# Last layer's dense experts on one Trainium2 core: the down product as three one-pass products on high and low parts, in two banks in turn

## The reference, cut to what matters

```
def _ffn(x, w1, b1, w2, b2):
    h = jax.nn.gelu(x @ w1.T + b1)          # 128 -> 512
    return h @ w2.T + b2                    # 512 -> 128
logits = xf @ router_w.T + router_b
routing = softmax(logits); sel_w, sel_idx = top_k(routing, 2); sel_w = sel_w / sel_w.sum()
comb = zeros_like(routing).at[rows, sel_idx].set(sel_w)
shared_out = _ffn(xf, shared_w1, shared_b1, shared_w2, shared_b2)
for each of 8 experts: acc = acc + comb[:, e] * _ffn(xf, w1_e, b1_e, w2_e, b2_e)
return shared_out + acc
```

## Time and profile before

| | |
|---|---|
| median of 3 runs | 1499.58 us |
| profiled execution, its own time | 1501.9 us |
| its span, first to last instruction | 1500.1 us |
| busy in the span: PE, DVE, ACT, POOL | 1155.9, 956.0, 681.9, 587.5 us |
| granted TensorE clock, mean of the span | 0.875 |
| down products (L1748), 288 matmul records | 152.1 us busy |
| up products (L1826), 432 matmul records | 217.8 us busy |

### The profile page before, as it was taken

How to read it: one execution, slowest core, us unless ns; L and a number is a source line. 1 busy time by engine, 2 the same in 40 slices (tenths; PEclk the granted TensorE clock), 3 DMA queues, 4 the chain that set the end, 5 groups by cost and what they waited for, 6 DMA issues and landing times.

```text
span 1500.1 us, 12998 instructions
## 1 busy us (share of the span) xinstructions
PE 1155.9 (77%) x3838; PEld 562.7 (38%) x3850; DVE 956.0 (64%) x2178; ACT 681.9 (45%) x1299; POOL 587.5 (39%) x404
## 2 busy tenths in 40 slices
PE   3226758859695959679697777878997899999897
PEld 1002323323232323324233433535454455555553
DVE  5976789688977788565857778665636634433321
ACT  6424543375436553152323525425553358554443
POOL 1880676328551767112103654363524111112111
PEclk7556778979697979769798999989998899999999
DMA  5000000000000000200001000000000200000000
GB/s 201 0 0 1 0 1 0 1 0 1 1 0 1 0 1 1 96 0 0 0 1 63 2 1 1 1 0 1 0 2 0 64 1 1 7 1 8 1 8 7
DMA packets 11270, 17.76 MB, mean 12 GB/s; under 512 B 1304, under 2 KB 7584, under 8 KB 10688
## 3 DMA queue, kind: packets, MB, share of 16 engines
q1 hardware_dynamic: 11200, 16.93, 3.4%
HBM read 15.88 MB, written 1.05 MB: 11 GB/s over the span
## 4 chain that ended last, share of the span: by engine, by line
PE 40%; DVE 11%; ACT 4%; issue 3%; POOL 2%; POOLq 0%; DVEq 0%; ACTq 0%
PE bankE L1748 8%; PE bankE L1826 6%; PE bankE L1247 3%; PE bankS L1790 2%; PE bankE L1309 2%; PE bankS L1775 2%; PE bankE L1268 1%; PE bankE L601 1%; PE bankS L1728 1%; DVE c_tw L1918 1%; PE bankE L523 1%; PE bankE L560 1%; ACT b_pr L1145 1%; PE bankE L1297 1%; PE bankE L594 1%
## 5 line engine op out<-in xcount | busy, mean ns | idle before, releaser
L1748 PE MATMUL bankE<-c_h,c_w 128*128 128x512 f32 x288 | 152.1, 611 | 8.2 <-DVE c_tw L1918 5.8
L737 DVE TENSOR_TENSOR_SCAN hs<-dA,carry,bankS 128x512 f32<-128x512 f32 x128 | 156.6, 1264 | 2.6 <-ACT dA L391 0.4
L1721 ACT ACTIVATE c_h<-bankE,C 128x512 f32<-128x512 f32 x144 | 98.8, 687 | 121.8 <-PE bankE L1826 121.4
L330 POOL TENSOR_TENSOR hc<-hs,cb 128x1024 f32<-128x1024 f32 x56 | 131.8, 2353 | 56.2 <-DVE hs L737 54.1
L307 POOL TENSOR_TENSOR cv<-cv,hc 128x1024 f32<-128x1024 f32 x56 | 132.3, 2362 | 4.4
L1617 POOL TENSOR_TENSOR c_acc<-c_acc,c_tw 128x512 f32<-128x512 f32 x32 | 40.8, 1274 | 186.6 <-DVE c_tw L1918 186.5
L1918 DVE SCALAR_TENSOR_TENSOR c_tw<-bankE,C,wb_ready 128x512 f32<-128x512 f32 x32 | 24.0, 751 | 129.3 <-PE bankE L1748 129.3
L424 ACT ACTIVATE sg<-bankE,C 128x512 f32<-128x512 f32 x80 | 54.7, 687 | 106.6 <-PE bankE L560 106.3
L1826 PE MATMUL bankE<-c_fH,c_w1H 128*128 128x512 f32 x144 | 101.6, 705 | 0.0
L729 DVE TENSOR_TENSOR bankS<-dx,bankS 128x1024 f32<-128x1024 f32 x64 | 78.4, 1225 | 6.0 <-PE bankS L489 5.3
L391 ACT ACTIVATE dA<-dl,Aneg 128x512 f32<-128x512 f32 x128 | 81.0, 709 | 2.2 <-DVE dl L720 2.2
(11 more groups left out here) (503 smaller groups left out, 2722.1 us busy)
## 6 DMA issues: line engine op xcount, KB each, us to landing
c_w<-in_w SPq DMA_DIRECT2D x1, 2304.0 KB, 8.7
X<-in_x SPq DMA_DIRECT2D x4, 256.0 KB, 4.0
wg<-in_gate_T SPq DMA_DIRECT2D x1, 1024.0 KB, 7.0
wu<-in_up_T SPq DMA_DIRECT2D x1, 1024.0 KB, 9.0
f<-in_w SPq DMA_DIRECT2D x1, 1024.0 KB, 7.2
out<-X SPq DMA_DIRECT2D x4, 256.0 KB, 2.3
b_wq<-in_Wqkv SPq DMA_DIRECT2D x1, 768.0 KB, 4.3
g<-in_sw SPq DMA_DIRECT2D x2, 256.0 KB, 3.5
```

The costliest lines, as they stand in the source:

```text
L330: pool.tensor_tensor(dst[:, :, :], hs[:, k % HS, :, :], cb[:, k % 2, :].unsqueeze(1).to_broadcast([P, HV, G]), ALU.mult).then_inc(s["hc_re ...
L737: V.tensor_tensor_scan(hs[:, k % HS, h, :], dA[:, (HV * k + q) % DA, :], dbx[:, h, :], carry[:, k, h:h + 1], ALU.mult, ALU.add).then_inc(s ...
L1721: act.activation(h[:, n % 3, :], E[k % 2][:, :], ACT.Gelu_apprx_tanh, bias=col("b1_3", k)).then_inc(s["c_h"], 1)
L1748: pe.matmul(E[2][:, :], w2[:, k, :], h[:, n % 3, :], start=(f == 0), stop=(f == FB3 - 1)).then_inc(s["c_down"], 1)
```

## The change

Four things are changed, all in lane c, and then the table.

1. The down product is made of three one-pass products of type fp32r, `(w2H, hH), (w2L, hH), (w2H, hL)`, in place of one product in fp32. `hH` is the high part of the Gelu's result and `hL` what is left. For even blocks ACT takes the Gelu twice, once rounded into `hH` and once into `h`; for odd blocks ACT takes it once and DVE rounds `h` into `hH`. DVE makes `hL = h - hH` for every block. POOL splits `w2` into `w2H` and `w2L` (pieces `s0` to `s8`, new), once for each expert and used by all groups.
2. The down product of a block stands two blocks behind its up product instead of one, and runs over the end of a group into the next one.
3. The down products of successive experts go to two banks in turn, `E[2]` and `S[3]`, so that one waits for `c_tw` of two experts before. `O1` turns into `E[3]` instead of `S[3]`, and the spread of the first routed expert stands at block 7 instead of 4.
4. Some semaphores are shared by several uses (`c_qkv` is now `inproj`, and the like), which changes no wait.

The core of the diff:

```
@@ last_layers, tensor @@
-        def down(g, k):
-            n = NU * g + k
+        def down(n):
+            g, k = divmod(n, NU)
             x_, f = divmod(k, FB3)
-            if n == 0:
-                pe.wait_ge(s["c_ld2"], 16)
-            pe.wait_ge(s["c_h"], n + 1)
-            if f == 0 and (g or x_):
-                pe.wait_ge(s["c_tw"], NX * g + x_)
-            pe.matmul(E[2][:, :], w2[:, k, :], h[:, n % 3, :], start=(f == 0), stop=(f == FB3 - 1)).then_inc(s["c_down"], 1)
+            if g == 0 and f == 0:
+                pe.wait_ge(s["c_split2"], 2 * x_ + 2)
+            pe.wait_ge(s["c_hL"], n + 1)
+            if f == 0 and NX * g + x_ > 1:
+                pe.wait_ge(s["c_tw"], NX * g + x_ - 1)
+            for q, (wp, hp) in enumerate(((w2H, hH), (w2L, hH), (w2H, hL))):
+                mm = pe.matmul(DOWN[(NX * g + x_) % 2][:, :], wp[:, k * P:(k + 1) * P], hp[:, n % 3, :], start=(f == 0 and q == 0), stop=(f == FB3 - 1 and q == 2))
+            mm.then_inc(s["fdown"], 1)
...
-                mm.then_inc(s["c_up"], 1)
-                if k > 0:
-                    down(i, k - 1)
-            elif p == "O0":
-                down(i, NU - 1)
+                mm.then_inc(s["up_ready"], 1)
+                if n >= 2:
+                    down(n - 2)
+            elif p == "O0" and i == NG - 1:
+                down(NU * NG - 2)
+                down(NU * NG - 1)
             elif p == "O1":
                 pe.wait_ge(s["c_acc"], (NX - 1) * (i + 1))
-                at_least(pe, s["c_done"], i, 1)
-                turn(S[3], acc_of(NX - 1)).then_inc(s["c_yt"], 1)
+                e3_next(s["c_done"], i + 1)
+                turn(E[3], acc_of(NX - 1)).then_inc(s["moT_ready"], 1)
@@ last_layers, scalar, piece U @@
+                act.wait_ge(s["up_ready"], N_U * NG + n + 1)
+                if n >= 3:
+                    act.wait_ge(s["fdown"], N_U * NG + n - 2)
+                if n % 2 == 0:
+                    act.activation(hH[:, n % 3, :], E[k % 2][:, :], ACT.Gelu_apprx_tanh, bias=col("b1_3", k)).then_inc(s["fs_ready"], 1)
+                act.activation(h[:, n % 3, :], E[k % 2][:, :], ACT.Gelu_apprx_tanh, bias=col("b1_3", k)).then_inc(s["fs_ready"], 1)
@@ last_layers, vector, piece U @@
-                if f == 0 and x_ > 0:
+                dve.wait_ge(s["fs_ready"], N_U * NG + kept(n + 1))
+                if n >= 3:
+                    dve.wait_ge(s["fdown"], N_U * NG + n - 2)
+                if n % 2:
+                    inc2(dve.tensor_copy(hH[:, n % 3, :], h[:, n % 3, :]))
+                    wait2()
+                dve.tensor_tensor(hL[:, n % 3, :], h[:, n % 3, :], hH[:, n % 3, :].bitcast(F32), ALU.subtract).then_inc(s["c_hL"], 1)
+                if f == 1 and x_ > 0:
                     weigh(i, x_ - 1)
@@ last_layers, gpsimd @@
+            elif p[0] == "s":
+                if k == 0:
+                    pool.wait_ge(s["c_ld2"], 16)
+                w = w2[:, k * FB3:(k + 1) * FB3, :].rearrange("p c n -> p (c n)")
+                high, low = (t_[:, k * FF3:(k + 1) * FF3] for t_ in (w2H, w2L))
+                pool.tensor_copy(high, w).then_inc(s["c_split2"], 1)
+                pool.wait_ge(s["c_split2"], 2 * k + 1)
+                pool.tensor_tensor(low, w, high.bitcast(F32), ALU.subtract).then_inc(s["c_split2"], 1)
@@ ORDER (a new table; the line in which the blocks of group 0 begin) @@
-    cR1.0 cy1.0 cW1.0 cR2.0 cR3.0 cV1.0 cX1.0 cQ0.1 cU0.0 cU1.0 cU2.0 cU3.0 cU4.0 cU5.0 cU6.0 cG0.1 cQ1.1 cU7.0 cU8.0 cU9.0 cU10.0 cU11.0
```

More of the change, by code:

```diff
@@ L355, in piece @@
                     at_least(act, s["tail_kept"], i, 1)
-                    act.activation(xm[:, h, KC - 1:], S[1 + h][:, :], ACT.Copy).then_inc(s["xm_ready"], 1)
+                    act.activation(xm[:, h, KC - 1:], S[1 + h][:, :], ACT.Copy).then_inc(s["proj_kept"], 1)
             elif p == "F0":
@@ L1556, in causal_layers, with last_layers @@
     return sync, gpsimd, scalar, tensor, vector
-def last_layers(s, X, C, col, S, E, ident, sel, half, dram, out, first_lane, second_lane, weights):
+def last_layers(s, X, C, col, S, E, ident, sel, half, dram, out, first_lane, second_lane, weights, spare):
     sb, sb2, sbw = first_lane.tensor, second_lane.tensor, weights.tensor
@@ L1588, in last_layers @@
     h = sb2("c_h", [P, 3, G])
+    hL = sb2("c_hL", [P, 3, G], F32R)
+    w2H = spare.tensor("c_w2H", [P, NU * D], F32R)
+    hH = spare.tensor("c_hH", [P, 3, G], F32R)
     wb, tw, acc = sb2("wb_ready", [P, 2, G]), sb2("c_tw", [P, 2, G]), sb2("c_acc", [P, 3, G])
@@ L1593, in last_layers, with kept @@
     w1, w1L = sbw("c_w1", [P, NU * P]), weights.over_last("c_w1L", [P, NU * P], F32R)
+    DOWN = (E[2], S[3])
+    SPREAD_AT = {2 * FB3 - 1: 1, **{FB3 * x_: x_ for x_ in range(2, NX)}}
+    def kept(n):
+        return n + (n + 1) // 2
     def acc_of(x_):
@@ L1656, in piece @@
                 x_, f = divmod(k, FB3)
-                if f == 1 and x_ > 1:
+                if f == 2 and x_ > 1:
                     add(pool, i, x_ - 1)
@@ L1681, in piece @@
                                                  (V[:, 0:4, :].rearrange("p a b -> p (a b)"), 0), (V[:, 4:8, :].rearrange("p a b -> p (a b)"), 1))):
-                    act.wait_ge(s["c_qkv"], 6 * i + n + 1)
-                    act.activation(dst, S[bank][:, :], ACT.Copy).then_inc(s["c_qkvc"], 1)
+                    act.wait_ge(s["inproj"], 4 * NG + 6 * i + n + 1)
+                    act.activation(dst, S[bank][:, :], ACT.Copy).then_inc(s["proj_kept"], 1)
             elif p[0] == "Z":
@@ L1813, in piece @@
                 x_, f = divmod(k, FB3)
[L1814 removed]
+                if k in SPREAD_AT:
+                    x_ = SPREAD_AT[k]
                     pe.wait_ge(s["w3_ready"], 2 * NG + i + 1)
@@ L1912, in weigh @@
                     dve.wait_ge(s["c_acc"], (NX - 1) * g)
-                dve.tensor_scalar(acc[:, 0, :], E[2][:, :], col("b2_3", 0), None, ALU.add).then_inc(s["c_tw"], 1)
+                dve.tensor_scalar(acc[:, 0, :], DOWN[NX * g % 2][:, :], col("b2_3", 0), None, ALU.add).then_inc(s["c_tw"], 1)
                 return
@@ L2118, in sandwich @@
         weights = Region(nc, WINDOW_END, SBUF[1])
-        lanes["c"] = last_layers(*shared, out, lorentz, last, weights)
+        lanes["c"] = last_layers(*shared, out, lorentz, last, weights, Region(nc, common.at, start))
         block = ctx.enter_context(nc.Block())
```

169 lines of the change are left out of this document (85 added, 84 removed).

## The result

The changed kernel takes 1507.36 us (median of 4 runs, 1505.71 to 1509.13) where the kernel before takes 1499.34 in the same comparison: a ratio of 1.006, interval 1.0048 to 1.0072. It is 8 us slower, where 13 us less was forecast. The profiled execution has a span of 1504.3 us.

The account below looks back on a forecast made before the run. PE was taken to bound the changed stretch, busy 93 to 97% of each group. The terms -23.0 - 16.8 + 19.2 + 6 + 1.2 gave -13.4 us, so 1486 us, own range 1476 to 1497, with rivals 1460 to 1502.

Parts of the forecast that it names:

- Part 5: New table, all lanes: same work, more table loads, at most 10 us; taken as 0, bounds -6 to +10.
- Part 2: Two banks for down products: the 0.48 us wait for c_tw goes at 35 turns, gaining 16.8 us.
- Part 1: Down product on PE: three one-pass products cost 0.69 instead of 0.86 us, gaining 23 us on 144 blocks.
- Part 3: Added DVE, ACT, POOL work fits, costing nothing alone; DVE and POOL collisions cost 19 us for sums, 6 for splits.
- Part 4: Tail and rest: last block's cast and subtraction unhidden, +1.2 us; second w2 load and O1 in E[3], 0.
- rival D: Down products on PE: weight loads do not hide, 49 us lost in place of 23 gained, 1558 us; chance 0.02.
- rival E: Lanes a and b: the table takes back eight table loads' worth, +10 us, 1496 us; chance 0.08.
- B: Groups 0 and 1 above all: DVE's attention waits reach PE through subtractions; at one half 1508 us; chance 0.12.
- C: POOL's sums and splits: every POOL instruction costs PE its whole length, +14, 1514 us; chance 0.05.
- A: DVE and POOL do not collide, or losses fall into slack: 1461 us; chance 0.21.
- the prediction's last sentence: The forecast fails as a whole if groups 0 and 1, half the blocks, behave unlike group 3, source of its prices.

Follow-up runs that it names:

- e6: e3 in the old table, with O0, O1, O2 moved behind blocks 1, 3, 6 and the turned total of groups 1 to 3 in S[0]: 1497.02 us.
- e8: The changed kernel in the old table, O0, O1, O2 behind blocks 1, 3, 6, turned total of groups 1 to 3 in S[0]: 1548.09 us.
- e2: The kernel before with the new table, without pieces s0 to s8 and with O0 still ahead of the next group's block 0: 1515.11 us.
- e3: The changed kernel with the old fp32 down product, without hH, hL, the second Gelu and the splits of w2: 1491.25 us.
- e5: The changed kernel with third product (w2H, hH) for (w2H, hL), one Gelu per block, no DVE casts or subtractions, splits kept: 1474.62 us.
- e4: The changed kernel with seven of POOL's eight sums of a group cut to one column: 1506.12 us.
- e9: e5 with DVE's 72 casts and 144 subtractions back, made from a weight in SBUF, so no down product waits for them: 1505.87 us.
- e11: e3 with the turned total in S[0]: 1488.16 us.
- e1: The changed kernel with the turned total at O1 put in S[0] instead of E[3]: 1503.31 us.

## Why the prediction was wrong, step by step

By the runs the change adds up as below. Each step is the difference of two medians. The table is undone first, then the banks, then the passes, and another order of steps would give other sizes: e6 and e8 show that the table's price depends on the products (from +16 to about -45 us).

| | forecast | measured |
|---|---|---|
| Part 5, table | 0 | +15.8 (e2) |
| Part 2, two banks and two behind (with the turn in `E[3]`) | -16.8 | -23.9 (e3) |
| Part 1 and the splits | -17 | -16.6 (e5) |
| Part 3, collisions of DVE with POOL's sums | +19.2 | 1.3 by e4, held in the rows below |
| Part 3, DVE's casts and subtractions by themselves | 0 | +31.3 (e9) |
| waiting for them, and the second Gelu | 0 | +1.5 (after) |
| Part 4, tail | +1.2 | 1.6 in the profiles, held in the rows above |
| sum | -13.4 | +8.1 |

The steps that failed are two that were priced at nothing: DVE's added work in Part 3 (13.6 us too little for the whole part) and the table in Part 5 (15.8 too little). Part 2 came out 7.1 us better than forecast and hid as much of it, which is luck in the number.

- **Part 1** held. Three passes 0.23 us apart, -23 and 6 for the splits; measured -16.6. Group 0 of e5 is 4.1 us shorter than that of e3 where 5.8 was due, so the splits may have taken some 2 us. No run without them was made, and the 4 us by which -16.6 falls short of -23 + 2 are not accounted for. The rule of the Trainium skill on weight loads (TensorE: Matmul & The Clock Gate, Part 3), rival D, is not borne out in the form in which the prediction took it: three loads in a row hide behind matmuls at 0.23. The same Part also lets a load run ahead that goes to the background weight buffer; the prediction left that case out, and the trace does not speak against it.
- **Part 2** was priced at -16.8, spread evenly over the experts. With two blocks behind it is -23.9 in the new table, of which 15.2 in group 0, and about -1 in the old: no price of its own. The mechanism is borne out where it was read, in groups 2 and 3, once the turn is out of `E[3]` (e11: 4.3 and 2.7 us).
- **Part 3** failed in the sentence "It fits too, so alone it costs nothing", and in the one it stands on, "Nothing on DVE held PE before but the weighing". The trace of before says otherwise, from 1179 us on:

```profile
PE bankE L1748 <- DVE c_tw L1918: 5.8, 17, 1.9
PE bankE L1809 <- DVE c_wt L2017: 5.2, 1, 5.2
PE bankE L1728 <- DVE c_xnE L1884: 3.2, 2, 2.2
PE bankS L1728 <- POOL c_acc L1617: 2.2, 1, 2.2
...
PE bankS L1728 <- DVE c_pT L1904: 1.5, 2, 1.1
```

  PE waited 9.9 us in these rows for the router's weights (`c_wt`), norms (`c_xnE`) and turned scores (`c_pT`), more than the 5.8 shown for the weighing, and nothing said what added work would do to them. The work was weighed against group 3's middle, where it does fit: 5.91 us per expert. I then priced only the collisions. They take 0.65 us of DVE's time per sum, and of the kernel's, where I had put 0.6, 0.05 by e4's time and at most some 0.4 with the clock's share: in the middle of group 3 nothing waits behind them. That 0.65 and 0.6 are alike is chance, as mine was a wait of PE. The added work itself was priced at 0 and costs 31 us, because DVE also makes the steps of chains on which PE waits: turned scores, the norms, the last weighing ahead of sum and turn. Each became later by the casts and subtractions ahead of it. My check compared sums, 165 us of DVE with 171 of PE for groups 0 and 1; a sum near the other engine's says nothing of a chain that goes back and forth between both.
- The Trainium skill (SBUF — State Buffer, Who interferes with whom) counts a cast among the instructions of DVE that can take the ports shared with POOL, and has whichever of the two comes second wait out the other's whole length. Here the cast that began at 1455.58 lay beside the sum for 1.03 us and lost 0.88 of it. The trace agrees, more closely than the earlier trace rows did, and e4 shows that the rule alone says little of the kernel's time.
- **Part 4**: the tail was +1.2, and is 15.0 us from the last up product on instead of 13.4. `O1` in `E[3]` was priced at 0 with the reason that five blocks cover the norm chain. That was the length of a norm of before, whose DVE had nothing else to do. PE waits 10.0 us for it, and it costs 4.1 (e1).
- **Part 5** failed too: 0, bounds -6 to +10; +15.8 with the old products, beyond the bound, and the largest miss of the sum in this order of steps. I looked for its price in table loads of lanes a and b, which end only 0.6 us later in the profiles, so rival E did not happen. What the traces show is that the chain from norm to first scores, which stood between blocks, stands ahead of block 0, where PE waits 13.3 us for its norms and the blocks begin 12 us later. That this is the cost is argued from the traces; no run has that piece alone moved back.
- **Rivals.** B gave 1508 us and the right engine, and its nearness to 1507.36 is luck. Its mechanism was that DVE's waits for the attention and the turned total (43.9 us) come through to PE by way of the subtractions. In the kernel after, from 1190 us on, DVE waits only 3.7 us for scores, 1.0 for PE's turned scores and 2.2 for the turned total, and the waits for `c_hL` give next to nothing back when they are taken away (e9). Even in the old table they are small (e8, 3.6 us). C gave 1514 for a reason that e4 refutes. A's sign of 5.8 to 5.9 us per expert appeared (5.82 to 5.91), and its view of the collisions was the nearer one, but its time did not appear. The forecast's own sign of subtractions whose longest is near 2 us came too (1.80, with a mean of 0.75), and says nothing of the kernel's time. The middle of group 3 was a poor judge, which the prediction's last sentence had feared.

Not settled: which moved piece of the table costs most, how much of e6's small gain is due to its changed O pieces, and what decides whether TensorE's clock falls behind a wait.
